# Loading three half-stacks by six channels a transfer instead of twelve, and the last results in four whole stores

## Time and profile before

| | |
|---|---|
| three runs | 231.95, 233.79, 235.48 us (median 233.79) |
| profiled execution | 230.8 us, of which the span in the trace is 228.9 us |
| mean granted TensorE clock | 0.993 of 2.4 GHz |
| PE busy | 210.9 us (92%) |
| DVE, ACT, POOL busy | 159.3, 137.0, 127.1 us |
| transfers | 12541 packets, 25.09 MB |
| the chain that ended last | 82% PE, 7% DVE, 4% issue, 2% POOL, 2% ACT, 1% DMA |

### The profile page before, as it was taken

How to read it: one execution, slowest core, us unless ns; L and a number is a source line. 1 busy time by engine, 2 the same in 40 slices (tenths; PEclk the granted TensorE clock), 3 DMA queues, 4 the chain that set the end, 5 groups by cost and what they waited for, 6 DMA issues and landing times.

```text
span 228.9 us, 8584 instructions
## 1 busy us (share of the span) xinstructions
PE 210.9 (92%) x3634; PEld 109.6 (48%) x3634; DVE 159.3 (70%) x284; ACT 137.0 (60%) x226; POOL 127.1 (56%) x165
## 2 busy tenths in 40 slices
PE   7779899999999999997799999999999987999980
PEld 4346666676757667665455444443333311222240
DVE  4677969698997989798755756344368789655332
ACT  3567676777859686763236333333346774898980
POOL 8245948466988869695989993223320000245433
PEclk9999999999999999999999999999999999999997
DMA  6950000120130464665637367777400001243312
GB/s 159 307 148 3 3 3 9 37 72 3 39 74 22 106 228 132 200 215 160 196 84 253 113 244 183 232 235 271 153 4 0 4 0 33 64 114 94 82 37 69
DMA packets 12541, 25.09 MB, mean 110 GB/s; under 512 B 6618, under 2 KB 8162, under 8 KB 10775
## 3 DMA queue, kind: packets, MB, share of 16 engines
q1 hardware_dynamic: 11606, 23.16, 33.6%
q0 software_dynamic: 896, 1.38, 2.7%
HBM read 18.63 MB, written 3.15 MB: 95 GB/s over the span
## 4 chain that ended last, share of the span: by engine, by line
PE 82%; DVE 7%; issue 4%; POOL 2%; ACT 2%; DMA 1%; POOLq 0%; DVEq 0%
PE psum L668 13%; PE psum L669 12%; PE psum L613 10%; PE psum L624 7%; PE psum L642 7%; PE psum L859 4%; PE psum L659 4%; PE psum L573 3%; PE psum L839 3%; PE psum L569 3%; PE psum L817 3%; PE psum L830 2%; PE psum L596 2%; PE psum L580 2%; PE psum L588 2%
## 5 line engine op out<-in xcount | busy, mean ns | idle before, releaser
L505 POOL TENSOR_TENSOR diff<-biased,mx 128x768 f32<-128x768 f32 x31 | 45.7, 1475 | 22.7 <-DVE mx L1146 22.7
L1277 DVE TENSOR_TENSOR gated<-psum,gel 64x512 f32<-64x512 f32 x32 | 22.1, 693 | 24.5 <-ACT gel L1030 24.5
L324 POOL DMA_DIRECT2D out<-yo x28 | 14.2, 515 | 44.2 <-DVE yo L1379 44.2
L1142 DVE TENSOR_TENSOR biased<-psum,pk 128x768 f32<-128x768 f32 x31 | 29.5, 952 | 11.2 <-PE psum L613 10.9
L1030 ACT ACTIVATE gel<-psum 64x512 f32<-64x512 f32 x32 | 18.9, 591 | 30.7 <-PE psum L669 30.6
L954 ACT ACTIVATE pt<-psum 128x768 f32<-128x768 f32 x32 | 25.9, 810 | 16.6 <-PE psum L624 16.4
L668 PE MATMUL psum<-sta,pk 108*128 108x512 f32 x64 | 33.7, 608 | 0.5 <-issue 0.5
L669 PE MATMUL psum<-stb,pk 108*128 108x512 f32 x64 | 32.7, 592 | 0.0
L1146 DVE TENSOR_REDUCE mx<-biased 128x12 f32<-128x768 f32 x31 | 29.5, 953 | 1.1
L613 PE MATMUL psum<-kmv,stq 32*64 32x192 f32 x512 | 28.1, 334 | 0.4 <-DVE biased L1154 0.3
L642 PEld LDWEIGHTS psum<-val,pt 128*32 128x32 f32 x1536 | 17.1, 110 | 12.4 <-issue 12.2
(11 more groups left out here) (108 smaller groups left out, 343.9 us busy)
## 6 DMA issues: line engine op xcount, KB each, us to landing
sta<-scratch SPq DMA_DIRECT2D x24, 288.0 KB
stb<-scratch SPq DMA_DIRECT2D x24, 288.0 KB
xtok<-xt SPq DMA_DIRECT2D x8, 192.0 KB, 4.2
xin<-xw SPq DMA_DIRECT2D x8, 192.0 KB, 5.5
x<-x1s SPq DMA_DIRECT2D x28, 48.0 KB
out<-yo POOLq DMA_DIRECT2D x28, 48.0 KB, 2.0
pk<-pack SPq DMA_DIRECT2D x1, 827.5 KB, 7.1
scratch<-ytok SPq DMA_DIRECT2D x4, 192.0 KB, 3.9
```

The costliest lines, as they stand in the source:

```text
L505: g.tensor_tensor(diff[:, t % 2].rearrange("q g w n -> q (g w) n"), scores_of, mx[:, t % 2].unsqueeze(2).to_broadcast([128, 4 * NH, WT]), ...
L1142: v.tensor_tensor(biased[:, slot].rearrange("q (p s) -> q p s", p=2), banks, wt("rpb").unsqueeze(1).to_broadcast([128, 2, 2 * NH * WT]), A ...
L1277: v.tensor_tensor(gated[64 * (b % 2):64 * (b % 2) + 64, b // 2, c * CH:(c + 1) * CH], bank(u % 4)[64:128], gel[:, u % 4, :], ALU.mult).the ...
```

## The change: what it does

`load_stack` gets a number of parts: for the first three halves, (0, 0), (0, 1) and (1, 0), each transfer is cut in two by channels, 6 channels and 18 partitions each, so that such a half is twelve transfers of 144 KB. The other five halves stay at six transfers of 12 channels and 36 partitions. The semaphore on which `edges` waits counts to 96 instead of 48 for the cut halves. The split of a row in the source's list of dimensions goes away, and with it an argument that was always False. At the end `store_last` goes away: SP waits until both halves of the last chunk are made and stores it whole, in four transfers of 48 KB.

```diff
-        def load_stack(queue, b, h, paced=False):
-
-            half = NT // 2
+        def parts_of(b, h):
+            return 2 if 2 * b + h < 3 else 1
+
+        def load_stack(queue, b, h):
+            parts = parts_of(b, h)
+            at, cols = NT // 2 * h, NT // 2
             for n in range(2):
                 c0, c1 = STACKS[n]
-                for y in range(3):
-                    if paced and (n or y):
-                        ...
-                    src = scratch[b]
-                    off = PAD + (y - 1) * W - 1 + c0 * NT + half * h
-                    src = bass.AP(src.tensor, src.offset + off, [[NT, c1 - c0], [1, 3], [half // 2, 2], [1, half // 2]])
-                    dst = stack(n, b)[y:RS:3, half * h:half * h + half].rearrange("p (q n) -> p q n", q=2)
-                    queue.dma_start(dst, src).then_inc(stack_in[n][b][h], 16)
+                wide = (c1 - c0) // parts
+                for part in range(parts):
+                    first = wide * part
+                    for y in range(3):
+                        src = scratch[b]
+                        off = PAD + (y - 1) * W - 1 + (c0 + first) * NT + at
+                        src = bass.AP(src.tensor, src.offset + off, [[NT, wide], [1, 3], [1, cols]])
+                        queue.dma_start(stack(n, b)[9 * first + y:9 * (first + wide):3, at:at + cols], src)\
+                            .then_inc(stack_in[n][b][h], 16)
@@ store_result
-            queue.wait_ge(yo_ready, c + 1)
+            queue.wait_ge(yo_ready, c + 1 if c < NCH - 1 else NCH + 1)
@@ store_last: removed
@@ sync, end
-            for half in range(2):
-                store_last(sp, half, range(B), last_stored)
-            sp.wait_ge(last_stored, 32 * B)
+            store_result(sp, NCH - 1, range(B), last_stored)
+            sp.wait_ge(last_stored, 16 * B)
@@ edges
-                    pool.wait_ge(stack_in[n][b][h], 48)
+                    pool.wait_ge(stack_in[n][b][h], 48 * parts_of(b, h))
```

More of the change, by code:

```diff
@@ L287, in store_y @@
                 queue.dma_start(half_of(0), ytok[64:128, 0, 0]).then_inc(done, 16)
-        def load_stack(queue, b, h, paced=False):
-            half = NT // 2
+        def parts_of(b, h):
[3 more added lines that the diff above has]
+            at, cols = NT // 2 * h, NT // 2
             for n in range(2):
                 c0, c1 = STACKS[n]
-                for y in range(3):
-                    if paced and (n or y):
-                        at, before = divmod(3 * n + y - 1, 3)
-                        queue.wait_ge(stack_in[at][b][h], 16 * (before + 1))
-                    src = scratch[b]
-                    off = PAD + (y - 1) * W - 1 + c0 * NT + half * h
-                    src = bass.AP(src.tensor, src.offset + off, [[NT, c1 - c0], [1, 3], [half // 2, 2], [1, half // 2]])
-                    dst = stack(n, b)[y:RS:3, half * h:half * h + half].rearrange("p (q n) -> p q n", q=2)
-                    queue.dma_start(dst, src).then_inc(stack_in[n][b][h], 16)
+                wide = (c1 - c0) // parts
[7 more added lines that the diff above has]
+                            .then_inc(stack_in[n][b][h], 16)
         def near_count(c):
@@ L325, in store_result @@
                     .then_inc(done, 16)
[L327 to L333, removed]
         block = ctx.enter_context(nc.Block())
@@ L398, in _ @@
                     wait_for_y(b)
-                    load_stack(sp, b, 0, False)
+                    load_stack(sp, b, 0)
                 if m in (5, 7):
-                    load_stack(sp, m // 2 - 2, 1, False)
+                    load_stack(sp, m // 2 - 2, 1)
             store_y(sp, 5)
```

## The result

The changed kernel takes 239.18 us in the median (238.49 to 243.15, four runs) against 232.87 us for the kernel before beside it; the ratio is 1.028, 95% interval 1.020 to 1.036. The changed kernel is slower by about 6.5 us; whether by more than 2% lies on the edge of the interval. The forecast was 241.8 us, with a range of 236.5 to 247.0.

The account below looks back on a forecast made before the run. PE's convolutions run back to back, with late loads, set by SP's program, just becoming the bound. Loads +9.0 and end -1.0 take 230.8 to 238.8; raised 3.0 to the median, 241.8 us, range 236.5 to 247.0.

Parts of the forecast that it names:

- Slower, through the loads, at `convolve(24)`: Late stack loads delay PE: (3, 0) masked at 169.8, `convolve(24)` at 169.9; the path is 9.0 us longer.
- the 3.0 us by which I had raised the forecast: Profiled execution lay 3.0 below the median of three runs, so 238.8 became 241.8.
- Lateness of (2, 0): Image 2's first load starts at 137.6 instead of 128.63, 9.0 us late, and everything to (3, 1) with it.
- Two terms of SP behind (1, 0): SP free of (1, 0) at 120.5; `store_y(4)` goes then, `store_x1(5)` ends at 126.1, when (1, 1) starts.
- Six engines, 134 GB/s: A transfer of six channels and 18 rows runs on six engines; a half takes 13.2 us instead of 6.6.
- This decides: In the first three halves, the number of DMA engines per transfer, six instead of twelve, decides the outcome.
- second rival: If six-channel transfers spread over other engines, (2, 0) starts 4.0 late; net +3.0, 236.8 us; chance 0.12.
- `wait_for_y(1)` and `residual(7)`: SP waits some 4 to 5 us for `store_y(3)`; `residual(7)` waits 4.5 us for `store_x1(5)`, PE stands 4.5 to 5.
- 3.6 us of waiting at `convolve(20)`: (2, 1) is masked at 162.0; `convolve(20)`, already 5 late, would start at 158.4 and waits 3.6 more.
- clock rival: After PE's stands at `turn_x1(7)` and `convolve(20)`, convolutions run at 1.2 GHz: 244.3, up to 247 us; chance 0.11.
- End, -1.0 forecast: Four whole stores replace eight issues; the last starts at 225.80 instead of 227.03, ending 1.0 us earlier.
- POOL's own stores of chunk 6 forbid more: At the end, POOL's stores of chunk 6 limit the gain to -1.0 us, ends -1.4 and +0.3.

Follow-up runs that it names:

- issues-alone run: All halves by twelve channels, whole stores at the end, a 192-byte transfer behind each of the first three halves' 18 transfers; ratio 1.022 to the kernel before.
- The runs of the two parts apart: Changed loads with the old end: ratio 1.024; all halves by twelve channels with the new end: 0.998, both against the kernel before.
- third buffer: The changed kernel with a third buffer of x1s, used by chunk 7 alone; ratio 1.035 to the kernel before.

## Why the prediction was right, step by step

- **Slower, through the loads, at `convolve(24)`: shown.** On the scale of the profiled execution I had 238.8, measured 238.7. That is luck: two of the terms, +9.0 at `convolve(24)` and -1.0 at the end, are off by 1.2 us each and cancel. In the median I had 241.8, measured 239.18: the 3.0 us by which I had raised the forecast, because the profiled execution lay that far below the median before, did not come again (238.7 against 239.18).
- **Lateness of (2, 0), +9.0 forecast, +7.4 measured; at `convolve(24)` +7.8.** Two terms of SP behind (1, 0) are mis-sized. The six-channel issue takes some 0.74 us with its gap (4.45 to 4.46 for the six of `sta`, mostly), not 0.79, so (1, 0) leaves SP after 8.9 us instead of 9.5. And I had let `store_y(4)` and `store_x1(5)` take SP the 5.6 us that they took before; they took 4.8 (119.68 to 124.49). From the first issue of (2, 0) to the masked (3, 0) it then took 0.4 us longer than before.
- **Six engines, 134 GB/s: shown** by the packets (11462), the share of 0.35 and the 137 GB/s. The Trainium skill, DMA: Bandwidth & Descriptors, "Rules for kernel authors", has two transfers to disjoint partition halves go over all 16 engines and only serialize; that does not hold for these shapes.
- **"This decides", of the engines: half right.** By the issues-alone run 3.0 of the 7.5 us at (2, 0) are issues. My second rival, only the issues count, I had priced at +3.0 in time; that part by itself measured 1.022, some 5 us of 231 (2.6 to 7.5). I had left the clock out of it, 1.4 us in its trace; another 1.6 us of that trace is its late start and not the issues. In time the engines' share on top is not resolved: 1.022 (1.011 to 1.032) and 1.028 (1.020 to 1.036) overlap.
- **`wait_for_y(1)` and `residual(7)`: shown**, 3.0 us of waiting and a stand of 4.52 us at PE, forecast 4 to 5 each. (1, 0) at 111.0 forecast, 110.79 measured.
- **3.6 us of waiting at `convolve(20)`: wrong**, it waits 0.01 us, and 1.84 at `convolve(24)`. The clock fell in the stand at `turn_x1(7)`, to 0.50 at 130 to 133, which made `convolve(4)` 3.3 us long instead of 1.7. So PE came to `convolve(20)` 1.3 us later than the 158.4 forecast, and (2, 1) was masked at 159.62, 2.4 us earlier than the 162.0 forecast: nothing was left to wait for. The clock rival's mechanism is real; in the changed kernel its cost lay inside the loads' lateness, as the rival had it for the first stand. In the traces where the stand comes at `convolve(20)` part of it is paid.
- **End, -1.0 forecast, nothing measured.** The stores went as worked out: four issues of 0.36 us from 232.28, and the last data through by 235.5, some 3.2 us after the last DVE operation, instead of 3.7. SP's part then ends at 235.9, 3.6 us after that operation, instead of 4.2. But SP does not end the span. Every engine closes with a DRAIN (L69), and POOL's, behind its stores of chunk 6, ends last. Before the change, then after (ns min/median/max, first and last start in us):

```profile
L69 POOLq DRAIN  x1: 3618/3618/3618, 225.1 to 225.1; - x1
L69 SPq DRAIN  x1: 13/13/13, 228.7 to 228.7; - x1
```

```profile
L69 POOLq DRAIN  x1: 3859/3859/3859, 232.8 to 232.8; - x1
L69 SPq DRAIN  x1: 7/7/7, 235.9 to 235.9; - x1
```

  Before, POOL's ends at 228.7, level with SP; after, at 236.7, and SP has come 0.8 us earlier for nothing. The runs of the two parts apart agree: with the old end POOL's DRAIN ends at 236.2 and SP's starts at 236.4, with the new end they are at 228.7 and 227.9. So the step that failed is "POOL's own stores of chunk 6 forbid more": POOL's end behind these stores forbade all of it. What POOL's DRAIN waits for the profile does not show.

Left open: the time from the first issue of (2, 0) to the masked (2, 1) runs from 22.9 to 26.2 us over the profiles that keep `store_y(5)` behind (1, 1), with the same transfers in the same order. Windows of 10 us in this stretch show nearly the same DMA share, 0.75 to 0.78, at 210 to 286 GB/s. I did not find what sets it.

## What to carry to other kernels

Before cutting a transfer, look at what its outermost dimension becomes: fewer rows can mean fewer engines (here six instead of twelve), and a small store behind it in the same queue then lands late (here `store_y(3)`, 7.77 us from issue to landing). Follow the one small store that a wait stands on, not the big loads: here the first two halves were masked some 22 us after their first issue and had slack, and the y behind them had none. What comes last at the end is also to be read engine by engine: SP's saving went into a wait for POOL. And when taking away one of two delays changes nothing, take away both before dropping the theory.

## What I had not expected of the hardware

What a stand of PE costs in clock depends on what comes behind it. In the changed kernel the slow products stand at `turn_x1(7)`, ahead of a wait for a stack, and lie inside that wait. With the third buffer the long stand, 6.17 us, comes at `convolve(20)`, and the clock is at 0.50 for the first products behind it (a window; then POOL's masks of `stb` for (2, 1) and (3, 0), and `convolve(24)`):

```profile
161.00:165.00 4.00, 3.83 (x5) 1.79 (x6) 0.00 (x0) 0.04 (x1) 0.92 (x4) 0.50 0.79 256
```

```profile
159.76 1.31 POOL L492 TENSOR_SCALAR stb<-stb,pk 108x64 f32<-108x64 f32 x3 [3.20 <-DMA stb<-scratch]
...
167.60 1.31 POOL L492 TENSOR_SCALAR stb<-stb,pk 108x64 f32<-108x64 f32 x3 [2.22 <-DMA stb<-scratch]
```

```profile
170.17 1.02 PE L667 MATMUL psum<-sta,pk 108*128 108x512 f32 x2
```

(3, 0) is masked at 168.91, and `convolve(24)` starts 1.3 us behind it instead of 0.1. That the whole kernel is slower for it is not shown: the spans are 238.3 and 236.9, but (2, 1) was also masked 1.4 us later in this trace (161.07 against 159.62), and the two ratios overlap.

A tiny transfer of six rows and 192 bytes takes SP 0.64 us to issue, almost as much as one of 288 KB (0.76).
